# An attention and gated feed-forward layer on one core: the scratch layout of Q and K, the first stack on two queues, the last low half on VectorE

## The reference

```python
x: (8, 512, 256); 16 heads of 16; Wq, Wk, Wv: (16, 256, 16)
q, k, v = x @ W + b                       # for each head
probs = softmax(q @ k.T * 16**-0.5 + causal)
x = layernorm(x + (probs @ v) @ Wo + bo)
gate = silu((x @ fp8(gate_w)) * gate_scale)       # 256 -> 768
up = (x @ fp8(up_w)) * up_scale
x = layernorm(x + ((gate * up) @ fp8(down_w)) * down_scale)
```

## Time and profile before

| what | value |
|---|---|
| median of 3 runs | 548.2 us (544.59 to 549.78) |
| the profiled execution | 545.57 us |
| its span | 543.8 us |
| granted TensorE clock, mean | 0.992 |
| PE busy | 522.4 us, 96% |
| DVE, ACT, POOL busy | 453.9, 320.5, 233.6 us |
| DMA packets | 47885, 66.63 MB |

### The profile page before, as it was taken

One profiled execution on the slowest core, in us unless ns is written; L12 is line 12 of the kernel. 1 busy time (PEld: TensorE's weight loads), 2 busy tenths in 40 slices (PEclk: granted clock), 3 DMA queues, 4 the chain that ended last, 5 costly groups with the idle time before them and its releaser, 6 DMA issues.

```text
span 543.8 us, 10823 instructions
## 1 busy us (share of the span) xinstructions
PE 522.4 (96%) x3954; PEld 355.0 (65%) x3955; DVE 453.9 (83%) x811; ACT 320.5 (59%) x595; POOL 233.6 (43%) x262
## 2 busy tenths in 40 slices
PE   8788999999999999999999999999999999999994
PEld 3544456565566655656656665565578888888894
DVE  7688668898888888889889889898848888988886
ACT  3247767657676676766767666667744454346432
POOL 6314333363254334436325433523444554455453
PEclk9989999999999999999999999999999999999998
DMA  5936594484557448347455553800000101110012
GB/s 184 244 81 206 155 298 153 148 251 146 164 191 213 155 138 229 130 140 220 122 177 166 150 177 119 213 7 4 1 0 2 40 0 40 40 39 12 29 40 79
DMA packets 47885, 66.63 MB, mean 123 GB/s; under 512 B 6488, under 2 KB 40152, under 8 KB 47832
## 3 DMA queue, kind: packets, MB, share of 16 engines
q1 hardware_dynamic: 46712, 63.84, 38.5%
q10 hardware_dynamic: 1120, 2.10, 1.4%
HBM read 37.62 MB, written 28.04 MB: 121 GB/s over the span
## 4 chain that ended last, share of the span: by engine, by line
PE 84%; DVE 5%; DMA 3%; issue 3%; ACT 1%; POOL 1%; ACTq 0%; SPq 0%; POOLq 0%; DVEq 0%
PE ps L1118 16%; PE ps L1062 11%; PE ps L1070 11%; PE ps L954 11%; PE ps L1240 8%; PE ps L1043 7%; PE ps L1023 5%; PE ps L1044 5%; PE ps L962 4%; DVE nmax L701 2%; PE ps L995 2%; PE ps L1006 2%; DMA q_st<-m_scratch 1%; PE ps L1088 1%; PE ps L1125 1%
## 5 line engine op out<-in xcount | busy, mean ns | idle before, releaser
L701 DVE TENSOR_REDUCE nmax<-ps 128x2 f32<-128x1024 f32 (+1 forms) x192 | 196.6, 1040 | 49.0 <-PE ps L1044 48.3
L510 ACT ACTIVATE probs<-ps 128x512 f32<-128x512 f32 x320 | 184.0, 597 | 70.5 <-PE ps L1062 68.8
L416 POOL TENSOR_SCALAR_AFFINE_SELECT probs<-probs 128x512 f32<-128x512 f32 x128 | 87.0, 694 | 184.7 <-ACT probs L510 184.7
L1062 PE MATMUL ps<-q_st,k_st 98*128 98x384 bf16 (+3 forms) x512 | 121.7, 301 | 5.5 <-ACT probs L510 3.7
L452 POOL TENSOR_TENSOR f_l<-f_full,f_h 128x512 fp32r<-128x512 f32 (+1 forms) x54 | 64.5, 1198 | 72.9 <-ACT f_h L602 72.7
L1043 PE MATMUL ps<-k_st,q_st 98*128 98x256 bf16 (+2 forms) x384 | 81.5, 273 | 4.5 <-DMA k_st<-k_scratch 2.7
L1044 PE MATMUL ps<-k_st,q_st 124*128 124x128 bf16 x512 | 83.8, 220 | 0.0
L1070 PE MATMUL ps<-probs,v_st 128*32 128x512 f32 (+3 forms) x1024 | 82.5, 438 | 0.0
L1062 PEld LDWEIGHTS ps<-q_st,k_st 98*128 98x128 bf16 x512 | 43.8, 98 | 49.9 <-issue 26.9
L595 ACT ACTIVATE sgate<-ps,s_gate 128x512 f32<-128x512 f32 (+1 forms) x54 | 34.2, 638 | 59.8 <-PE ps L1118 59.8
L1044 PEld LDWEIGHTS ps<-k_st,q_st 124*128 124x128 bf16 x512 | 45.9, 97 | 18.8 <-DVE nmax L701 13.7
(11 more groups left out here) (102 smaller groups left out, 841.3 us busy)
## 6 DMA issues: line engine op xcount, KB each, us to landing
q_st<-q_scratch SPq DMA_DIRECT2D x28, 384.0 KB
k_st<-k_scratch SPq DMA_DIRECT2D x28, 384.0 KB
q_scratch<-part SPq DMA_DIRECT2D x14, 384.0 KB, 2.6
k_scratch<-part SPq DMA_DIRECT2D x14, 384.0 KB, 2.8
xT<-in_attn_xT SPq DMA_DIRECT2D x8, 512.0 KB, 4.0
q_scratch<-part SPq DMA_DIRECT2D x16, 256.0 KB, 2.9
k_scratch<-part SPq DMA_DIRECT2D x16, 256.0 KB, 2.1
resid<-in_attn_x SPq DMA_DIRECT2D x8, 512.0 KB, 5.5
```

The lines of the kernel that those rows point to most:

```text
L416: pool.affine_select(out=blocks, in_=blocks, compare_op=ALU.is_ge, fill=0.0, base=0, pattern=[*pattern, [1, P]], channel_multiplier=-1).th ...
L510: act.activation(probs[:, u, :], ps[:, u % 2, :], ACT.Exp, scale=SCALE).then_inc(exp_done, 1)
L701: dve.tensor_reduce(nmax[:, i, heads[0]:heads[-1] + 1], src, AX.X, ALU.max, negate=True).then_inc(max_taken, 1)
L1062: m = pe.matmul(ps[:, u % 2, c0:c0 + T - P * j], k_st[0:RP, g, h, P * j:P * j + P], q_st[0:RP, g, h, P * j:T], start=True, stop=True)
```

## The change

The third dimension of the scratch tensors becomes the group, so that a group's 16 rows of one part are 64 KB in one piece; the host permutes the columns of Wq and Wk (and the biases) to match. `load_stack` is split into `load_q` and `load_k` and reads `scratch[t, :, g % 2]`, with dimensions (6 parts, 16 rows, 4 heads, 512), where it read 96 rows with one stride. In entry 0 `load_k(1, 0)` comes after `load_mrow(0, 2)`. The first stack's third DMAs (q and k) go to ACT's queue, ahead of two part copies, and the first two of each to SP's; SP waits for the stack before it stores parts 2 and 3. V's last projection is cut in two. The low half of the last chunk is computed on DVE; the last two row blocks' matmuls signal one by one, and DVE takes them one by one. `gate_up(0, 3)` goes ahead of `transpose_yn(B - 1, 1)`.

```diff
-    q_scratch = nc.dram_tensor("q_scratch", (2, NP, D, H // 2, T), ...
+    q_scratch = nc.dram_tensor("q_scratch", (2, NP, 2, D, HG, T), ...
...
-        def load_first(eng, stack, scratch, parts, g):
-            row = RM
-            for run in parts:
-                src = scratch[g // 2, run[0]:run[-1] + 1, :, HG * (g % 2):HG * (g % 2) + HG, :].rearrange("a d h t -> d a h t")
+        def load_first(eng, stack, scratch, parts, g, first=0, last=2):
+            row = RM + D * sum(len(run) for run in parts[:first])
+            for run in parts[first:last + 1]:
+                src = scratch[g // 2, run[0]:run[-1] + 1, g % 2].rearrange("a d h t -> d a h t")
...
+            def load_rows(n, g, stack, scratch, k):
+                t = g // 2
+                sp.wait_ge(st_full, NU * (G * (n - 1) + g + 1))
+                sp.wait_ge(part_stored[k], parts_count(n))
+                sp.dma_start(stack[RM:RP, g], scratch[t, :, g % 2]).then_inc(stack_loaded[g], 16)
...
             def load_stack(n, g):
-                t, heads = g // 2, slice(HG * (g % 2), HG * (g % 2) + HG)
-                sp.wait_ge(st_full, NU * (G * (n - 1) + g + 1))
-                for stack, scratch, k in ((q_st, q_scratch, 2 * t), (k_st, k_scratch, 2 * t + 1)):
-                    sp.wait_ge(part_stored[k], parts_count(n))
-                    sp.dma_start(stack[RM:RP, g], scratch[t, :, :, heads, :].rearrange("a d h t -> (a d) h t")).then_inc(stack_loaded[g], 16)
-                sp.dma_start(q_st[0:RM, g], zero_rows[:, :].unsqueeze(1).to_broadcast([RM, HG, T])).then_inc(stack_loaded[g], 16)
+                load_q(n, g)
+                load_k(n, g)
...
-            load_first(sp, q_st, q_scratch, FIRST_Q, 0)
+            load_first(sp, q_st, q_scratch, FIRST_Q, 0, 0, 1)
+            sp.wait_ge(mask_filled, 3)
+            sp.wait_ge(part_stored[1], parts_count(0))
+            load_first(sp, k_st, k_scratch, FIRST_K, 0, 0, 1)
+            sp.wait_ge(stack_loaded[0], stack_count(0))
             first_parts(2)
             first_parts(3)
...
                 store_mrow(n, 2)
                 if nxt:
-                    load_stack(n + 1, 0)
+                    load_q(n + 1, 0)
+                if n and nxt:
+                    load_k(n + 1, 0)
                 load_mrow(n, 2)
+                if not n:
+                    load_k(1, 0)
...
             for m in (2, 3):
                 hi_part(0, m, MX + m)
+            act.wait_ge(mask_filled, 2)
+            act.wait_ge(part_stored[0], parts_count(0))
+            load_first(act, q_st, q_scratch, FIRST_Q, 0, 2)
+            act.wait_ge(mask_filled, 3)
+            act.wait_ge(part_stored[1], parts_count(0))
+            load_first(act, k_st, k_scratch, FIRST_K, 0, 2)
             for m in (2, 3):
                 mid_part(0, m, probs[:, m, :])
-            act.wait_ge(mask_filled, 3)
-            act.wait_ge(part_stored[1], parts_count(0))
-            load_first(act, k_st, k_scratch, FIRST_K, 0)
...
+            def last_f_lo():
+                n, j = B - 1, 2 * IC - 1
+                ic, cols = chunk(n, j)
+                dve.wait_ge(fhi_ready, n * IC + j + 1)
+                dve.tensor_tensor(f_l[:, n % 2, ic, cols], f_full[:, j % 3, 0:WIDTH[n]], f_h[:, n % 2, ic, cols].bitcast(F32),
+                                  ALU.subtract).then_inc(flo_last, 1)
+            def last_out(tb):
+                dve.wait_ge(down_last, tb - 1)
+                dve.tensor_tensor(y_sum[:, tb, :], ps[:, LAST[tb - 2], 0:C], s_down[:], ALU.mult).then_inc(last_scaled, 1)
+                dve.wait_ge(last_scaled, tb - 1)
+                dve.tensor_tensor(y_sum[:, tb, :], y_sum[:, tb, :], resid_v[:, B - 1, tb, :], ALU.add).then_inc(last_summed, 1)
+                dve.wait_ge(last_summed, tb - 1)
+                dve.bn_stats(stats[:, tb, :], y_sum[:, tb, :]).then_inc(st2_ready, 1)
...
-            sum_out(B - 1, 1)
-            out_stats(B - 1, 1)
+            last_f_lo()
+            last_out(2)
+            last_out(3)
...
-                if u == 1:
-                    project_v(1, 1, None, 1)
-                elif u > 1:
-                    if u == 2:
+                if u in (1, 2):
+                    project_v(1, 1, u - 1, 1)
+                elif u > 2:
+                    if u == 3:
...
             transpose_y(W - 1)
+            gate_up(0, 3)
             transpose_yn(B - 1, 1)
-            gate_up(0, 3)
             project_o(B - 1, 0)
```

More of the change, by code:

```diff
@@ L41, in layer @@
     NM = 6
-    q_scratch = nc.dram_tensor("q_scratch", (2, NP, D, H // 2, T), BF16, kind="Internal").ap()
-    k_scratch = nc.dram_tensor("k_scratch", (2, NP, D, H // 2, T), BF16, kind="Internal").ap()
+    q_scratch = nc.dram_tensor("q_scratch", (2, NP, 2, D, HG, T), BF16, kind="Internal").ap()
+    k_scratch = nc.dram_tensor("k_scratch", (2, NP, 2, D, HG, T), BF16, kind="Internal").ap()
     m_scratch = nc.dram_tensor("m_scratch", (G, TB, RM, HG, P), BF16, kind="Internal").ap()
@@ L166, in layer @@
         gu_full, sg_ready, f_ready = sem("gu_full"), sem("sg_ready"), sem("f_ready")
-        fhi_ready, flo_ready = sem("fhi_ready"), sem("flo_ready")
+        fhi_ready, flo_ready, flo_last = sem("fhi_ready"), sem("flo_ready"), sem("flo_last")
+        down_last, last_scaled, last_summed = sem("down_last"), sem("last_scaled"), sem("last_summed")
         down_full, down_out = sem("down_full"), sem("down_out")
@@ L249, in part_rows @@
             def part_rows(n, k, a, b, step=1):
-                return (q_scratch, k_scratch)[k % 2][k // 2, a:b:step].rearrange("a d h t -> (d h) a t")
+                return (q_scratch, k_scratch)[k % 2][k // 2, a:b:step].rearrange("a g d h t -> (g d h) a t")
             def first_parts(k):
@@ L275, in store_parts, with load_q, load_k @@
                     sp.dma_start(part_rows(n, k, 0, 3), part[:, k, :, :]).then_inc(part_stored[k], 16)
-            def load_stack(n, g):
-                t, heads = g // 2, slice(HG * (g % 2), HG * (g % 2) + HG)
-                sp.wait_ge(st_full, NU * (G * (n - 1) + g + 1))
-                for stack, scratch, k in ((q_st, q_scratch, 2 * t), (k_st, k_scratch, 2 * t + 1)):
-                    sp.wait_ge(part_stored[k], parts_count(n))
-                    sp.dma_start(stack[RM:RP, g], scratch[t, :, :, heads, :].rearrange("a d h t -> (a d) h t")).then_inc(stack_loaded[g], 16)
-                sp.dma_start(q_st[0:RM, g], zero_rows[:, :].unsqueeze(1).to_broadcast([RM, HG, T])).then_inc(stack_loaded[g], 16)
+            def load_rows(n, g, stack, scratch, k):
[3 more added lines that the diff above has]
+                sp.dma_start(stack[RM:RP, g], scratch[t, :, g % 2]).then_inc(stack_loaded[g], 16)
+            def load_q(n, g):
+                load_rows(n, g, q_st, q_scratch, 2 * (g // 2))
+                sp.dma_start(q_st[0:RM, g], zero_rows[:, :].unsqueeze(1).to_broadcast([RM, HG, T])).then_inc(stack_loaded[g], 16)
+            def load_k(n, g):
+                load_rows(n, g, k_st, k_scratch, 2 * (g // 2) + 1)
+            def load_stack(n, g):
+                load_q(n, g)
+                load_k(n, g)
             def store_mrow(n, g):
@@ L467, in _ @@
                 f_lo(n + 1, IC - 1)
-            for j in range(IC, 2 * IC):
+            for j in range(IC, 2 * IC - 1):
                 f_lo(B - 1, j)
@@ L765, in _ @@
                 first_rest(k + 1)
+                if k:
+                    fill_mask(dve, k_st, mask_k, k).then_inc(mask_filled, 1)
                 first_lo(k)
                 first_lo(k + 1)
-                dve.wait_ge(pool_const, 6 + 2 * MG)
-                fill_mask(dve, k_st, mask_k, k).then_inc(mask_filled, 1)
+                if not k:
+                    dve.wait_ge(pool_const, 6 + 2 * MG)
+                    fill_mask(dve, k_st, mask_k, k).then_inc(mask_filled, 1)
             for w in range(2):
@@ L855, in sum_out @@
                 y = y_sum[:, 2 * v:2 * v + 2]
[L856 to L860, removed]
+                dve.tensor_tensor(y, ps[:, DOWN + v, :].rearrange("p (b c) -> p b c", b=2),
                                   s_down[:].unsqueeze(1).to_broadcast([P, 2, C]), ALU.mult).then_inc(down_out, 1)
@@ L1257, in last_down @@
                 for ic in range(IC):
-                    pe.wait_ge(flo_ready, n * IC + IC + ic + 1)
+                    if ic + 1 < IC:
+                        pe.wait_ge(flo_ready, n * IC + IC + ic + 1)
+                    else:
+                        pe.wait_ge(flo_last, 1)
                     for tb in (2, 3):
@@ L1262, in last_down @@
                                           start=ic == 0 and f is f_h, stop=ic == IC - 1 and f is f_l)
-                m.then_inc(down_full, 1)
+                        if ic + 1 == IC:
+                            m.then_inc(down_last, 1)
             gate_up(0, 2)
             transpose_y(W - 1)
+            gate_up(0, 3)
             transpose_yn(B - 1, 1)
-            gate_up(0, 3)
             project_o(B - 1, 0)
@@ L1303 @@
```

(4 more changed lines are left out.)

## The result

The change made the kernel slower: 610.7 us in the median of six runs (607.6 to 613.9), where the kernel before took 546.4 us beside it (543.6 to 550.8). The ratio is 1.120, with a 95% interval of 1.115 to 1.124. The prediction said 553 us, between 541 and 565. So the direction was right, and the size was not: +64 us instead of +8. The profiled execution took 613.9 us, with a span of 612.2 us.

The account below looks back on a forecast made before the run. It took PE, busy in 96% of the span, as the bound, so edits count through its idle time. Terms: 545.6 - 3.9 + 11.7 (waits behind six-engine loads) = 553.4 us, given as 553, range 541 to 565.

Parts of the forecast that it names:

- The count of engines: Stack loads with 6 parts outermost run on six DMA engines, 16 rows each, where 16 had 6 rows each.
- Rival (1): All 16 engines still take the stack loads, so only the other terms count: 541.7 us; chance 0.25.
- The price of a place: Maxima load behind a whole stack pair: PE waits 0.9 us at each of 13 places, +11.7 us.
- the third: Highest bound for the 13 places: at 0.31 us a row, 4.6 us of wait each, +60 us.
- Rival (3): Six engines and a full queue, other units wait too: 1.7 us or more at 13 places, 564 and above; chance 0.15.
- Rival (2): Six engines, but the slack covers them: 0 to 0.3 us at 13 places, 542 to 546 us; chance 0.2.
- The sum of the rest: Start, third unit, change-over and tail, all terms but the layout's loads: -3.9 us together.
- Start: First stack's loads and V's projection: PE resumes at about 18.6 us, not 21.08; -2.6 us, between -0.5 and -3.2.
- Third unit: First entry's third unit: the maxima load, with K's load now behind it, no longer makes PE wait; -1.1 us.
- Change-over: Passage to the feed-forward part: the gap only moves behind the transposes; 0, between -0.1 and +0.1 us.
- Tail: After the last chunk: low half on DVE -0.2 us, row blocks one by one -0.2 us, between -0.4 and +0.1.

Follow-up runs that it names:

- e1: The changed kernel with the source of the stack loads walked with d (16) outermost instead of the 6 parts: 542.2 us, 0.995 of before.
- e2: The changed kernel with the old layout of the Q and K scratch tensors, their stores, loads and weight order: 542.1 us, 0.995 of before.
- e4: The changed kernel with 12 unused matmuls before PE's wait for the maxima at first and third groups: 589.3 us, 1.082 of before.
- e7: e1 with the first stack, the parts' order and V's projection as before the change: 541.7 us, 0.990 of before.
- e10: The same kernel as e7, measured again beside e9 in more executions: 543.7 us, 0.996 of before.
- e3: The kernel before with only the new layout and its loads: 609.5 to 623.8 us, median 621.3; 609.5 us is the time to compare.
- e9: The same kernel as e1, measured again beside e10 in more executions: 541.6 us, 0.990 of before.
- e5: The changed kernel with each stack load cut into two DMAs with 8 values of d outermost, on eight engines: 558.1 us, 1.019 of before.
- e8: The changed kernel with x's load moved from behind group 0's maxima load to behind the next stack pair: 605.9 us, 1.108 of before.

## Why the prediction was right in kind and wrong in size

**The count of engines** was right: six, proven by the packets, by the share of 0.375 and by e1. Rival (1), all 16 engines, had 0.25 and fell. The sum of that rival, 541.7 us, is what e1 and e2 measure (542.2 and 542.1), so the kernel would have been 0.5% faster without this one step.

**The price of a place** failed, and it is the step that made the prediction wrong: "I take 0.9 us for each", 13 times, +11.7 us. The 13 places were the right ones, but had 3.2 us each in the mean. At the third group of entry 4 the working can be followed. The Q load is issued 4.44 us after the start of the unit before, as in the earlier trace rows. The pair's traffic begins some 5.9 us after it (predicted 5.3), lasts 6.3 us (predicted 6.1), and the maxima with their closing take 1.3 us more (predicted 0.6). The landing is at 13.4 us after the unit's start, where 12.0 was predicted and 11.2 wanted. No single term was far off: the row of 4 KB at 145 / 6 = 24 GB/s is 0.17 us, not even the 0.19 taken. The 1.3 us are 0.4 us for the maxima's rows (275.10 to 275.50 in the trace's packets, at the pair's end) and 0.8 until they count as landed. But once the landing is behind the unit's start, every further delay stands in full in the wait: 1.4 us late on a landing of 12.0 made 2.1 us out of 0.8. Two small terms were left out. SP's issues became longer (0.75 and 0.71 us instead of 0.37), and the zero rows' issue now stands between Q's and K's, so K's load is issued 1.67 us behind Q's instead of 0.52. And the traffic begins slowly (the DMA view from 269 to 270 us has 41 to 123 GB/s); that the one makes the other is not shown. At the first group of an entry about 1.0 us was taken; it was 2.7 to 5.6, 28.0 of the 42.2 us. There the load issued at 241.10 took 8.45 us. From 243.5 to 245.5 us all 16 engines are busy, with x's rows beside the pair's:

```profile
243.50:245.50 2.00, 2.00 (x24) 1.01 (x21) 1.89 (x9) 1.16 (x2) 1.75 (x3) 1.00 1.05 227
```

A 4 KB row that starts in this window takes 0.28 us in the mean of the trace's packets, where it takes 0.17 from 270 to 274 us. The sum had counted the load ahead of the pair, xT, and not the one behind it.

**The clock** is the step that was missing altogether. The prediction had the stalls at one microsecond and did not ask what PE's clock does after longer ones. e4 prices it at 21.4 us, a third of the loss. In the profiled spans, after is 72.2 us above e1 where the sum had 11.7 us: 44.0 us of it idle, 28.2 us busy, for which it had nothing. Of the bounds, only the third, "at 0.31 us, 4.6 us each, +60", came near the result. It had been set aside because six engines make no saturation. At the third groups the rows indeed took 0.17 us; at the first ones x's load brought the saturation for 2 us, but the waits were 3.2 us in the mean, not 4.6, and the clock made up the rest. Rival (3), "1.7 us or more at 13 places ... 564 and above", is what happened in kind at the 13 places, though hardly any other unit waited; its chance of 0.15 was too small, and the range stopped where it began.

**Rival (2)**, the slack covers it, fell: 6488 - 5929 small packets fewer, and 15 waits.

**The sum of the rest** was -3.9 us, and e1's span is 543.8 - 540.0 = 3.8 us below before's. But its terms were not all right. *Start*, -2.6: PE resumed at 19.43 us in e1 and 19.88 in the kernel after, not 18.6. In the latter the last K issue began at 15.99 instead of 15.6, and landed 3.75 us later, not 3.0. That "nothing else is under way" did not mean free engines: from 16.4 to 19.8 us their share is 1.04, at 225 GB/s. (The 3.4 us "with a busy queue" are not there: rows 3 have 4.20; a landing of 3.4 us is that of the maxima load of the earlier trace rows.) The chain of the kernel after, and DVE's maxima, which do run without the gap of the earlier trace rows:

```profile
15.99 3.75 DMA k_st<-k_scratch
```

```profile
20.52 5.92 DVE L724 TENSOR_REDUCE nmax<-ps 128x2 f32<-128x1024 f32 x6 [1.17 <-PE ps L1084]
```

Unit 0 starts 2.1 us earlier in e1 than in before (30.79), but e7 and e10, with the start as before, have it at 29.52 and 29.69, so by these pairs 0.8 to 0.9 us are the edit's. Where the rest comes from is not shown; e3, with before's start as well, has 30.29. The lead is given back by unit 8. *Third unit*, -1.1: right. From unit 1 to unit 2 it was 44.74 to 55.04, 10.3 us, and is 41.46 to 50.47, 9.0 us, with no wait for the maxima in e1. (With six engines it is back, 1.44 us.) In e1's timeline:

```profile
50.47 0.38 PE L1102 MATMUL ps<-q_st,k_st 98*128 98x512 bf16 x1
```

Another 1.2 us of e1's lead there, within unit 0, are no gain: the profiled execution of before had PE at the half clock from 37.3 to 40.7 us, and e2's had it from 36.2 to 39.7, with all of the change but the layout. *Change-over*, 0: right. From `transpose_y` to `project_o` there were 394.80 to 398.64, 3.84 us; in e1 there are 391.18 to 394.96, 3.78 us. The gap of the earlier trace rows has moved behind the transposes and is as long. In e1's timeline:

```profile
394.33 0.58 ACT L521 ACTIVATE ynT<-ps 128x512 f32<-128x512 f32 x1
...
394.96 1.99 PE L1063 MATMUL ps<-w_o,ynT 128*128 128x256 f32 x8 [0.88 <-ACT ynT L521]
```

*Tail*, -0.2: right. From the last `f_h` on ACT to the last `norm_out` on DVE there were 534.80 to 540.54, 5.74 us, and are 531.22 to 536.74, 5.52 us. DVE's low half took 0.43 us, near the 0.45 guessed for it. In e1's timeline:

```profile
531.67 0.43 DVE L942 TENSOR_TENSOR f_l<-f_full,f_h 128x256 fp32r<-128x256 f32 x1
532.75 0.42 DVE L948 TENSOR_TENSOR y_sum<-ps,s_down 128x256 f32<-128x256 f32 x1 [0.64 <-PE ps L1304]
```

So 3.8 us against 3.9 was luck in part: 0.9 us of the start, a half-clock stretch of before and landings that vary stood in for a term of 2.6 us.

## What to carry to other kernels

When a DMA's source or destination gets another shape, count its outermost dimensions first, and then its closing packets: contiguous bytes gave nothing here, and the order of two dimensions was worth 68 us. Where a slack is nearly used up, a range must be built from what happens beyond it and not from the point estimate's neighbourhood: once the landing is late, each further delay counts in full at every place, and waits of two microseconds and more on PE can add a half-clock stretch each. Count what is issued behind a load as well as what is ahead of it. The best kernels of this study are the change with d outermost, with either start, and with the old layout (e1, e2, e7, e9 and e10, 0.990 to 0.996 of before); they can't be told apart.

## What the runs showed of the hardware that was not expected

**The clock falls for stalls of some microseconds.** 13 stretches of 3.4 or 6.8 us at 1.2 GHz came with waits of 1.9 to 5.6 us, in a kernel whose PE is busy for 90%. The length of the wait alone doesn't sort them: the 2.12 us before 276.33 were followed by one, the 2.5 us of e5's longest wait weren't, and in e8 a wait of 1.82 us was followed by one and another of 2.07 us wasn't. The Trainium skill, "TensorE: Matmul & The Clock Gate", section "HAM oscillation — how this bites in real kernels", tells of a kernel in which a wait for DMA in each tile let the clock fall each time; the kernel after shows the same at 13 places, and e4 that unused matmuls in the wait prevent it, at all 12 places that had them.

**The shape of a DMA sets how many engines it has.** 96 rows in one dimension had 16, the same 96 rows as 6 times 16 had six, and as 16 times 6 sixteen again. The Trainium skill, "DMA: Bandwidth & Descriptors", section "Why a DMA increments its semaphore by 16 and not by 1", has the rule for the number of engines, and every run agrees: 6 for the changed loads, 16 with d outermost, and eight for e5's halves, whose closing packets (two DMAs of 8) are as many as those of one on sixteen: 6489 small packets. The maxima load, on two engines by the earlier trace rows, had to wait until a pair on six was through (275.10 us), so its two are among the six.

**The shape of a DMA also has a price on the queue that issues it.** A stack load's issue on SP took 0.30 to 0.43 us in most cases with one joined dimension (before; two of 0.37 in the earlier trace rows), 0.55 to 0.60 us with d outermost (e1) and 0.70 to 0.76 us on six engines (two of them in the timeline above). For e1's loads that costs nothing that can be measured: its time is e2's, whose loads have one joined dimension.
